# Moving the store of groups gathered ahead from SyncE's queue to GpSimd's, with 23 groups ahead in place of 30

## The reference

```python
xn = _layernorm(x, axis=-1)
# edge attention: features of the source node, a softmax over the edges of each destination
e = leaky_relu((el[src]*mask + er[dst]*mask + em*mask summed over T) / 3)
rst = segment_sum(feat_src[src] * softmax_by_dst(e), dst)
# linear attention over all nodes: softmaxed q and k, context = k^T v, out = q context, @ Wout, layer norm
x = x + rst + mix(xn)
x = x + moe_ffn(layernorm(x))      # 8 experts, three layers each, all computed, weighted by a softmax
```

## Time and profile before

| What | us |
|---|---|
| Median of 3 runs | 3389.73 (3389.61 to 3389.95) |
| The profiled execution's own time | 3383.94 |
| Its span, first to last instruction | 3382.3 |
| POOL gathers ahead (first gather to start of the last) | 96.7 to 442.5 |
| First instruction of SP in the edge phase | 450.38 |
| POOL gathers in the edge phase | 454.2 to 2416.3 |
| First load of the last phase | 2468.09 |

### The profile page before, as it was taken

How to read it: one execution, slowest core, us unless ns; L and a number is a source line. 1 busy time by engine, 2 the same in 40 slices (tenths; PEclk the granted TensorE clock), 3 DMA queues, 4 the chain that set the end, 5 groups by cost and what they waited for, 6 DMA issues and landing times. The chain is left out here.

```text
span 3382.3 us, 76670 instructions
## 1 busy us (share of the span) xinstructions
PE 2979.6 (88%) x21350; PEld 2402.1 (71%) x21351; DVE 2641.9 (78%) x4924; ACT 1699.5 (50%) x5754; POOL 2077.2 (61%) x3347
## 2 busy tenths in 40 slices
PE   7995648889898888998988889888859999999999
PEld 4564537777676767776766677676648888888899
DVE  4574548889888888988988889888857777777786
ACT  4651216556555555665655566555543433333343
POOL 2888878888888888888888888888500000000000
PEclk9997769999999999999999999999879999999999
DMA  7567876666666666666666666666331000100000
GB/s 270 182 209 242 304 239 198 183 181 193 194 187 184 184 195 191 187 187 196 193 182 182 202 184 191 183 194 188 98 98 42 20 20 23 37 20 17 17 21 10
DMA packets 285469, 509.70 MB, mean 151 GB/s; under 512 B 84049, under 2 KB 186870, under 8 KB 277508
## 3 DMA queue, kind: packets, MB, share of 16 engines
q0 software_dynamic: 86032, 287.41, 29.8%
q1 hardware_dynamic: 198900, 220.45, 20.6%
q10 hardware_dynamic: 384, 0.00, 0.0%
HBM read 415.38 MB, written 92.29 MB: 150 GB/s over the span
## 5 line engine op out<-in xcount | busy, mean ns | idle before, releaser
L978 POOL DMA_INDIRECT gat<-scratch_table,idx x1376 | 1332.0, 968 | 231.6 <-issue 226.8
L1337 PE MATMUL ps_s<-msg,oh 128*128 128x272 f32 x4000 | 1055.9, 414 | 41.4 <-DVE msg L1183 26.3
L1337 PEld LDWEIGHTS ps_s<-msg,oh 128*128 128x128 f32 x4000 | 758.5, 197 | 198.1 <-ACT tmp L1044 42.1
L1053 ACT ACTIVATE acc<-acc,sc 128x33 f32<-128x33 f32 x2000 | 458.8, 339 | 230.4 <-DVE acc L1171 230.4
L1580 POOL DMA_DIRECT2D out<-y x13 | 9.8, 756 | 899.6 <-DVE y L1794 899.6
L1183 DVE TENSOR_TENSOR msg<-gat,ps_m 128x2048 f32<-128x2048 f32 x250 | 559.2, 2276 | 0.0
L1627 ACT ACTIVATE h<-ps_h,fsh,fsc 128x512 f32<-128x512 f32 (+1 forms) x416 | 290.8, 750 | 508.9 <-PE ps_h L1840 508.9
L1044 ACT ACTIVATE tmp<-ps_s,sc 128x33 f32<-128x33 f32 x2000 | 384.4, 304 | 17.2
L140 POOL MEMSET rest_e<- 128x192 f32 x1376 | 388.3, 282 | 0.7
L1033 ACT CAST oh<-ps_o 128x1024 f32<-128x1024 bf16 x250 | 259.1, 1037 | 143.4 <-PE ps_o L1277 122.4
L1670 DVE CAST h_hi<-h 128x1024 fp32r<-128x1024 f32 (+1 forms) x208 | 137.2, 660 | 201.7 <-ACT h L1627 201.5
(11 more groups left out here) (217 smaller groups left out, 5406.1 us busy)
## 6 DMA issues: line engine op xcount, KB each, us to landing
d16r<-scratch_dst SPq DMA_DIRECT2D x250, 256.0 KB
scratch_ahead<-stage SPq DMA_DIRECT2D x30, 1152.0 KB, 4.8
gat<-scratch_ahead POOLq DMA_DIRECT2D x30, 1152.0 KB
scratch_acc<-acc SPq DMA_DIRECT2D x250, 136.0 KB
gat<-scratch_table,idx POOLq DMA_INDIRECT x1376
edge<-in_edge SPq DMA_DIRECT2D x250, 88.0 KB
scratch_table<-trow POOLq DMA_DIRECT2D x49, 144.0 KB, 4.1
xin<-in_x SPq DMA_DIRECT2D x49, 128.0 KB, 4.4
```

The costliest lines, as they stand in the source:

```text
L978: pool.indirect_dma_start(out=gat[:, s, c, :], out_offset=None, in_=scr["table_rows"], in_offset=bass.IndirectOffsetOnAxis(ap=idx[:, g * C ...
L1053: act.mul(acc[:, new, cols], acc[:, old, cols], sc[:, j, 0, h:h + 1]).then_inc(scaled, 1)
L1337: last = pe.matmul(ps_s[j][:, 0:SUMS], oh[:, s, j, c, :], msg[:, 2 * (s % 2) + j, c, :], start=(c == 0), stop=(c == C - 1), skip_group_che ...
```

## The change

POOL stores each group itself. The store of group i - 1 stands behind the third gather (c == 2) of group i, in the place of that gather's rest; the last one follows the last gather, and POOL then waits until all stores have landed. The stores, their waits and the final waits go from SP's queue. PRE falls from 30 to 23, so AHEAD has 23 groups, again spread evenly, and the edge phase gathers 179 groups instead of 172.

```diff
-PRE = 30
-EARLY = 18
+PRE = 23
+HALFWAY = 2
...
-            def store_ahead(i):
-                sp.wait_ge(staged[i % 2], 16 * C * (i // 2 + 1))
-                sp.dma_start(scr["ahead"][i], stage[:, i % 2, :, :].rearrange("p c n -> p (c n)")) \
-                    .then_inc(ahead_out[i % 2], 16)
-
-            for i in range(EARLY):
-                store_ahead(i)
             sp.wait_ge(er_step, 5)
...
-            turns = dict(zip(range(5, NT, 4), range(EARLY, PRE)))
-            tiles(sp, (reload, 0), (store_mix, 3), unrolled=True, at={t: partial(store_ahead, i) for t, i in turns.items()})
-            for i in range(EARLY + len(turns), PRE):
-                store_ahead(i)
-            for i in range(2):
-                sp.wait_ge(ahead_out[i], 16 * len(range(i, PRE, 2)))
+            tiles(sp, (reload, 0), (store_mix, 3), unrolled=True)
...
+            def store_ahead(i):
+
+                pool.wait_ge(staged[i % 2], 16 * C * (i // 2 + 1))
+                pool.dma_start(scr["ahead"][i], stage[:, i % 2, :, :].rearrange("p c n -> p (c n)")) \
+                    .then_inc(ahead_out[i % 2], 16)
+
             def gather_ahead(i):
...
-                    rests.after(pool, c)
+                    if c == HALFWAY and i > 0:
+                        store_ahead(i - 1)
+                    else:
+                        rests.after(pool, c)
 
             for i in range(PRE):
                 gather_ahead(i)
+            store_ahead(PRE - 1)
+            for i in range(2):
+                pool.wait_ge(ahead_out[i], 16 * len(range(i, PRE, 2)))
```

## The result

The changed kernel takes 3417.61 us (median of three runs, 3417.46 to 3422.70), the kernel before 3389.73. The ratio is 1.0087, with a 95% interval of 1.0064 to 1.011: slower by 28 us, where 3.3 were forecast. The profiled execution took 3417.61 us with a span of 3415.7, against 3382.3 before, so between the two traces lie 33.4 us, and that is the difference the rows have to explain.

A forecast was written before the change was run, and what follows sets the result against it. POOL's gather stream was taken to bound the edge phase and set both phase ends. Node phase -69.9 and edge phase +73.2 gave +3.3 us on 3389.73, so 3393.0 us, range 3386 to 3406.

The forecast's parts named there:

- part 1: Node phase, POOL's end: with 23 groups and 22 stores on POOL, POOL would allow the next phase at 377.1 us.
- I keep it: Node phase, POOL's end: 6.5 us from the end of the gather period to the next phase, taken over unchanged.
- part 3: Edge phase: seven more groups to gather cost 77.8 us, seven fewer loads save 4.6 us; loss 73.2 us.
- 56 x 1.39: Edge phase: 56 added gathers on POOL at 1.39 us each with rest, 77.8 us.
- What bounds the kernel: Both phases: POOL's gather stream sets both ends; the edge phase is as long as POOL's work in it.
- Rival (b): POOL's stores in the node phase are dear through stalls: 20 us on POOL's end, sum +19.9, 3410 us; chance 0.08.
- Part 2: Node phase, mix loop's end: start at 288, last tile done at 374.9, next phase at 380.5; gain 69.9 us.
- the pace of 1.80: Mix loop: 1.80 us a tile, from nine intervals at the loop's start; called the uncertain term.
- rival (a): Mix loop ends the node phase, PE at 1.2 GHz needing 2.14 us a tile: sum +19.6, 3409 us; chance 0.22.
- clearly less than 73: Sign of a wrong forecast: the edge phase growing by clearly less than 73 us.
- (c): Edge phase takes less than the added gathers: loses 49 us instead of 73, sum -21, 3369 us; chance 0.08.
- (d): Node phase change does nothing for the mix loop, which ends near 443 again: sum +73, 3463 us; chance 0.02.

## Why the prediction was wrong

Two steps failed: in part 1 "I keep it", which carried the end of POOL's path over unchanged and cost about 8 us, and in part 3 the price "56 x 1.39" of the added gathers, which was too low by about 21 us. The mechanism, gathers moved from a node phase that shrinks to an edge phase that POOL bounds, was right.

**What bounds the kernel** was read rightly. POOL's stream sets the edge phase: 1432 gathers, no wait for a buffer, and 50.9 us from its last gather to the last phase, 51.8 before; and 56 gathers more made the phase longer by at least their own time. PE's waits for POOL rose to 163.6 us, 36 of them, where about 180 us stood.

**Part 1, POOL's end.** The gathers were right to a microsecond: the last begins at 370.00. The store on POOL was priced from the load of the same size, and this is one of the 23, with the gathers beside it:

```profile
111.56 0.95 POOL L433 DMA_INDIRECT stage<-scratch_table,pidx  x1 [0.16 <-issue]
112.51 0.59 POOL L425 DMA_DIRECT2D scratch_ahead<-stage  x1
113.41 0.97 POOL L433 DMA_INDIRECT stage<-scratch_table,pidx  x1 [0.30 <-issue]
```

0.90 us lie between the end of one gather and the next, against the 0.82 that were taken, or 1.8 us over 22 stores. No store was held up: all 23 took 582 to 602 ns, as the row of their line says:

```profile
L425 POOL DMA_DIRECT2D scratch_ahead<-stage x23: 582/589/602, 112.5 to 375.2; - x23
```

The first step that failed is the last one of this part, "I keep it": 6.5 us from the end of the gather period to the next phase, carried over from a kernel in which SP waited for the landing and POOL had been done. Measured are 17.7 us (371.4 to 389.05): 3.8 until the store is issued, since its group must have landed, 4.7 until it has landed and POOL's list is at its end, 8.64 of drain, and 0.6 for the change of phase. Rival (b) has the same hole: it put a price on each store but none on the end. It is 11.2 us of POOL's path, which thereby passed the mix loop's.

**Part 2, the mix loop.** The row of its first finished tile, against the earlier trace rows:

```profile
290.24 0.49 DVE L688 SCALAR_TENSOR_TENSOR kexp<-mixo,rstd,xre 128x256 f32<-128x256 f32 x1 [5.32 <-DMA xre<-in_x]
```

290.24 where 288 was forecast, and the last tile begins at 376.69 and is done at 377.2, where 374.9 was forecast, so (376.69 - 290.24) / 48 = 1.80 us a tile, to the digit. The window of the loop (us, busy of PE, PEld, DVE, ACT, POOL, then clock, DMA share, GB/s), against the earlier trace rows:

```profile
290.00:372.00 82.00, 60.63 (x260) 43.70 (x260) 65.30 (x225) 27.08 (x89) 69.69 (x109) 0.96 0.99 338
```

The stretch before from which the pace of 1.80 was taken had this window:

```profile
316.00:334.00 18.00, 12.91 (x51) 10.12 (x52) 13.91 (x48) 5.67 (x18) 15.89 (x26) 0.77 0.96 321
```

The granted clock was 0.96 now, so rival (a), PE at the lower clock, didn't come about; and the pace was the same at 0.77 and at 0.96, so PE's clock didn't set it. The DMA share was 0.96 and 0.99, which points to the transfers as the limit, but no run tests that. The last tile was done 2.3 us late, nearly all from the later start, but SP needed only 3.5 us behind it for the last landing, where the forecast had 5, and was done at 380.6. With the 0.2 us from SP's end to the next phase that the trace before shows, the loop alone would have let the next phase begin at 380.9. Of the 8.5 us by which the node phase was missed (380.5 to 389.05) 0.4 are thus the loop's and 8.1 are POOL's end. That the loop's end came out so well has a part of luck in it, two errors of about 2 us that cancel.

**Part 3, the edge phase,** is the larger miss: 73.2 us forecast, 94.0 measured. This is the second step that failed. "56 x 1.39" priced each gather at one interval between two gathers without disturbance. By the rows above, gathers were 12.1 us longer than 56 undisturbed ones, and the gaps 11.1 us longer; the rests, the loads and the two ends of the phase made 2.4 less. The trace before doesn't hold this excess: its own means, 0.968 for a gather, 0.165 for a gap and 0.282 for a rest, make 1.415 us, or 79.2 instead of 77.8. The gaps are the pauses that come with the new spacing, shown by the run that set it back (-8.7 us of gaps, -6.6 of the phase). For the longer gathers no cause was found. Part of them may not be owed to the seven groups at all: with 30 groups stored by POOL they were already 5.6 us busier than before (1337.6 against 1332.0), and equal gathers differ by 7.4 us between two executions. The forecast named only "clearly less than 73" as the sign of an error here; it came from the other side. That seven groups cost 12 to 13 us each (84.0 and 90.6 us by their spacing) and save about 11 (75.9 us of node phase, POOL storing in both) is what the runs with POOL's stores show; whether it is so with SP's stores as well was measured only on the slow chips.

**The rivals.** (a) is out by the pace of 1.80 at a clock of 0.96. (b) is out by the store's row: the Trainium skill (SBUF — State Buffer, section "SBUF: two separate sides") has descriptor writes of GpSimd locked out in the two-port modes of DVE, and with DVE busy 80% of the mix loop no store took over 602 ns. The trace doesn't show which of DVE's operations ran in such a mode; for these stores the rule cost nothing that can be seen. Gathers of over 952 ns, up to 1332, are what it may have on them, and no run here tells. The time it gave, 3410, is nearer to the result than the forecast, by luck, since the cause was another. (c) and (d) are out by +94.0 and by the mix loop at 376.7.

**The sum by measured terms:** node -61.3, edge +94.0, last phase +0.7, together +33.4 us between the profiles; the runs differ by 28, since the profiled execution of the kernel before was 5.8 us below its median and that of the changed kernel wasn't. By parts: storing on POOL with 30 groups +18 (14.5 and 3.4), going from 30 to 23 groups another +15 (-75.9 and +90.6). The medians give 14.2 for the first, and 6.9 for the second at the old spacing; the +18 is larger because the profiled execution of the kernel before was a short one. Neither part pays for itself on these chips, and none of the versions that ran there beat the kernel before.

## What to carry to other kernels

When a wait is moved to another engine, price that engine's end of block too, its last landing and the drain behind it: what counts is whose drain ends last, not who arrives last; "the rest stays as it is" holds only while the same engine closes the phase. When work is moved in a stream that bounds a phase, one clean interval gives a lower bound, and here the old trace's mean would hardly have been better (10.7 us a group against 10.5, and 12 to 13 measured): a changed list of instructions can have pauses that the old one has not, so leave room above the forecast. And a queue that holds stores behind a wait for a slow result (SP's, behind `er`) is hidden as long as that result is early; on chips where it was late, the same order cost 116 to 127 us in one wait.

## What the runs showed of the hardware

The drain of GpSimd at the end of the block has a length that goes with the program and can repeat to the nanosecond. Where POOL had nothing else left to do, it took 8643 ns in all four traces with all of 23 groups stored by POOL, also on a slow chip and with half of the rests, and 5703 ns in all three with 30 groups. In the kernel before it took 4.04 us, 2.7 of them behind POOL's last instruction, and 8.6 behind it with 22 stores on POOL and the last one on SP. What sets the length isn't known, only that it doesn't grow with the number of stores and doesn't need POOL to have waited for a landing.

With 23 groups spread over the whole phase POOL paused 1.0 to 1.2 us between a memset and the next indirect DMA, 13 times, nine or ten groups apart, with no wait of the kernel open. The pauses stood ahead of the same 13 gathers with the stores on POOL or on SP, on a fast chip or, with one of them shorter, on a slow one. With the 23 groups at the spacing of one in seven there were four, of 0.8 us, behind the last loaded group, and in the two kernels with 30 groups, on chips like the first, none.

And one program took 3388 to 3395 us in three comparisons and 4278 to 4423 us on two other chips (one of these two gave 4278 once, and 4404 and 4421 later), with ACT idle 7 to 8 us at a time in the records and another engine as the bound: there the ranking of the versions was another one.
